# Moving the sum of two scaled token projections from VectorE to GpSimd in a fused decoder kernel

## The reference

```python
A = minimum(-softplus(dd_A), -A_FLOOR);  dt = softplus(dd_dt + dt_bias);  tr = sigmoid(trap)
theta = cumsum(tanh(angles) * dt * pi)            # one angle per head and rotated feature
def step(carry, (dt, A, tr, th, b, c, x)):        # over the 128 tokens
    alpha = exp(A * dt);  beta = (1 - tr) * dt * alpha;  gamma = tr * dt
    base = b * (px * beta + x * gamma)            # px is x of the token before
    sr = sr * alpha + [base[:R] * cos(th), base[R:]];   si = si * alpha + base[:R] * sin(th)
    y = sum((sr[:R] * cos(th) + si * sin(th)) * c[:R]) + sum(sr[R:] * c[R:])
out = (y + D * x) * silu(z) @ w_out.T
x1 = layernorm(u + out)
```

## Time and profile before

| | before |
|---|---|
| time, median of 3 runs | 638.13 us (637.15 to 638.27) |
| span of the profiled execution | 639.7 us |
| the seven groups that start at 46.4 us and end at 206.6 us | 160.2 us |
| mixer's last group, from 206.6 us to the end of its block | 19 us |
| attention and experts | from 226 us to 639.7 us |
| busy over the whole span: PE, DVE, ACT, POOL | 90%, 75%, 44%, 32% |

### The profile page before, as it was taken

One profiled execution on the slowest core, in us unless ns is written; L12 is line 12 of the kernel. 1 busy time (PEld: TensorE's weight loads), 2 busy tenths in 40 slices (PEclk: granted clock), 3 DMA queues, 4 the chain that ended last, 5 costly groups with the idle time before them and its releaser, 6 DMA issues. The chain is left out here.

```text
span 639.7 us, 17897 instructions
## 1 busy us (share of the span) xinstructions
PE 578.3 (90%) x6280; PEld 482.1 (75%) x6280; DVE 480.6 (75%) x1174; ACT 279.9 (44%) x548; POOL 205.7 (32%) x256
## 2 busy tenths in 40 slices
PE   5769998999999856998999999788999999999994
PEld 5647876777787645787788877576888888888884
DVE  2858878977988758686787788675887887887863
ACT  2356645645755423564575564353233233233220
POOL 4233214314412574324445547732021021020122
PEclk9969999999999976998999999899999999999998
DMA  7123122112111363445445645000010000110000
GB/s 223 61 68 86 40 66 66 36 63 66 53 55 40 106 190 105 132 138 148 140 131 149 166 117 168 13 5 34 1 34 2 33 33 0 33 33 0 18 18 16
DMA packets 43086, 46.13 MB, mean 72 GB/s; under 512 B 5056, under 2 KB 31328, under 8 KB 43024
## 3 DMA queue, kind: packets, MB, share of 16 engines
q1 hardware_dynamic: 41104, 42.57, 22.8%
q0 software_dynamic: 704, 1.92, 1.0%
q10 hardware_dynamic: 1216, 0.79, 0.5%
HBM read 32.48 MB, written 10.94 MB: 68 GB/s over the span
## 5 line engine op out<-in xcount | busy, mean ns | idle before, releaser
L1957 PE MATMUL bank<-xT_hl_c,w_up 128*128 128x512 f32 x432 | 118.1, 409 | 2.4 <-ACTq L67 2.4
L141 POOL TENSOR_TENSOR rstd<-mv,norm_c 128x4 f32<-128x4 f32 x24 | 5.2, 216 | 292.4 <-DVE mv L135 189.1
L1282 DVE TENSOR_REDUCE nmax<-bank 128x4 f32<-128x512 f32 x112 | 72.0, 685 | 22.9 <-PE bank L1439 21.5
L1879 ACT ACTIVATE sg<-bank 128x512 f32<-128x512 f32 x72 | 43.0, 597 | 105.0 <-PE bank L1957 103.1
L1186 ACT ACTIVATE prob<-bank 128x512 f32<-128x512 f32 x128 | 69.4, 594 | 42.9 <-PE bank L1439 36.5
L1957 PEld LDWEIGHTS bank<-xT_hl_c,w_up 128*128 128x128 f32 x432 | 76.1, 189 | 15.8 <-ACTq L67 2.6
L1973 PEld LDWEIGHTS bank<-w_down,hid 128*128 128x128 f32 x576 | 74.4, 191 | 6.0 <-issue 0.5
L1973 PE MATMUL bank<-w_down,hid 128*128 128x128 f32 x576 | 75.6, 275 | 0.0
L1429 PE MATMUL bank<-neg_i,mask 64*128 64x256 bf16 x512 | 51.5, 280 | 9.6 <-issue 3.2
L1912 DVE TENSOR_TENSOR gu<-sg,bank 128x512 f32<-128x512 f32 x64 | 43.8, 685 | 21.4 <-PE bank L1957 11.4
L1916 DVE TENSOR_TENSOR hid<-gu,bank 128x512 f32<-128x512 f32 x64 | 44.0, 687 | 6.5
(11 more groups left out here) (220 smaller groups left out, 1192.3 us busy)
## 6 DMA issues: line engine op xcount, KB each, us to landing
rows<-sum_rows_scratch SPq DMA_DIRECT2D x32, 256.0 KB, 3.2
k_stack<-k_scratch SPq DMA_DIRECT2D x32, 128.0 KB, 2.8
q_stack<-q_scratch SPq DMA_DIRECT2D x32, 128.0 KB, 2.8
k_scratch<-k_part SPq DMA_DIRECT2D x16, 192.0 KB, 2.3
q_scratch<-q_part SPq DMA_DIRECT2D x16, 192.0 KB, 2.4
x<-xT_in SPq DMA_DIRECT2D x8, 256.0 KB, 8.2
mask<-mask_in SPq DMA_DIRECT2D x8, 256.0 KB, 3.0
xres<-x_in SPq DMA_DIRECT2D x8, 256.0 KB, 3.7
```

The source lines that it names most:

```text
L1282: dve.tensor_reduce(nmax[:, b, 4 * u:4 * u + 4], (SS0, SS1)[n % 2][:, :].rearrange("p (i k) -> p i k", i=4), AX_X, ALU.max, negate=True).t ...
L1879: act.activation(sg[:, k, :], GG[k][:, :], ACT.Silu).then_inc(a_s.sem, 1)
L1957: mm = pe.matmul(bank[:, :], w_up[:, which, a, c, :], xT_hl[par][:, v, :], start=(n == 0), stop=(n == 2))
```

## The change

The scaling of the two projections stays with DVE, but writes into one of two buffers (`xg` gets a second one); the sum of the halves, `w_tok`, is made by POOL, in a function `inputs_of` of its own. PE's `tokens` waits for the scaling, PE's `back` for POOL's sum. POOL's order becomes, in groups 0 to 6: `steps_of(g+2)` (groups 0 to 5), sum of block 2, masks of blocks 0 to 2 of group g+1, sum of block 3, mask of block 3, sums of blocks 0 and 1 of group g+1, then the norm of group g, and in group 6 the fill of the key stack. In group 7: sum of block 2, third part of the first keys, sum of block 3, the two other third parts. The rounded angles (`whole`) lose their buffer and lie in that of the sines (`trig`), with one more wait of DVE for its own `rotate` of the group before.

```diff
-        ang, whole, frac = sb("ang", [P, 2, GT]), sb("whole", [P, 2, GT]), sb("frac", [P, 2, GT])
+        ang, frac = sb("ang", [P, 2, GT]), sb("frac", [P, 2, GT])
         trig = sb("trig", [P, 2, GT])
+        whole = trig
...
-        s_w = sem("w_ready", 2 * GS)
+        s_xg, s_w = sem("xg_ready", GS), sem("w_ready", GS)
...
             dve.wait_ge(s_ang.sem, s_ang.at(g, 1))
+            dve.wait_ge(s_prod.sem, s_prod.at(g - 1, 3))
             dve.tensor_scalar(whole[:, :, :], ang[:, :, :], ROUND, -ROUND, ALU.add, ALU.add).then_inc(s_whole.sem, 2)
...
-        xg = sb("xg", [P, 2, D_INNER])
+        xg = sb("xg", [P, 2, 2, D_INNER])
...
+            def inputs_of(g, b):
+
+                pool.wait_ge(s_xg.sem, s_xg.at(g, b))
+                pool.wait_ge(s_y.sem, s_y.at(g, b - 2))
+                pool.tensor_tensor(w_tok[:, b % 2, :], xg[:, b % 2, 0, :], xg[:, b % 2, 1, :], ALU.add).then_inc(s_w.sem, 1)
+
             def group(g, par, left):
                 if left == 2:
                     steps_of(pool, g + 2)
-                if left:
-                    for b in range(GS):
+                inputs_of(g, 2)
+                if left:
+                    for b in range(GS - 1):
                         causal(pool, g + 1, b)
+                else:
+                    part_third(pool, a, 0, 1)
+                inputs_of(g, 3)
+                if left:
+                    causal(pool, g + 1, GS - 1)
+                    for b in range(2):
+                        inputs_of(g + 1, b)
                     if left == 2:
                         pool.wait_ge(s_frac.sem, s_frac.at(g + 2, 1))
                     normalise_pool(pool, g, s_res, s_x1, res, mv, rstd, norm_c, x1[:, bass.ds(g * GS, GS), :])
                 if not left:
-                    for group_, which in ((0, 1), (0, 0), (1, 1)):
+                    for group_, which in ((0, 0), (1, 1)):
                         part_third(pool, a, group_, which)
...
             for b in range(2, GS):
                 causal(pool, 0, b)
+            for b in range(2):
+                inputs_of(0, b)
             pairs(pool, group)
...
             def inputs_of(g, b):
 
                 dve.wait_ge(s_xx.sem, s_xx.at(g, b))
-                dve.wait_ge(s_w.sem, s_w.at(g, 2 * b - 1))
-                dve.tensor_tensor(xg[:, :, :].rearrange("p s (h e) -> p (s h) e", h=HEADS),
+                dve.wait_ge(s_w.sem, s_w.at(g, b - 2))
+                dve.tensor_tensor(xg[:, b % 2, :, :].rearrange("p s (h e) -> p (s h) e", h=HEADS),
...
-                                     [P, 2 * HEADS, HD]), ALU.mult).then_inc(s_w.sem, 1)
-                dve.wait_ge(s_w.sem, s_w.at(g, 2 * b))
-                dve.wait_ge(s_y.sem, s_y.at(g, b - 2))
-                dve.tensor_tensor(w_tok[:, b % 2, :], xg[:, 0, :], xg[:, 1, :], ALU.add).then_inc(s_w.sem, 1)
+                                     [P, 2 * HEADS, HD]), ALU.mult).then_inc(s_xg.sem, 1)
...
-                pe.wait_ge(s_w.sem, s_w.at(g, 2 * b - 4))
+                pe.wait_ge(s_xg.sem, s_xg.at(g, b - 2))
...
-                pe.wait_ge(s_w.sem, s_w.at(g, 2 * b + 1))
+                pe.wait_ge(s_w.sem, s_w.at(g, b))
```

More of the change, by code:

```diff
@@ L540, in _ @@
             def _(pool):
-                for s in (s_sel, s_turns):
+                for s in (s_sel, s_turns, s_w):
                     s.prime(pool)
@@ L618, in link @@
                     dve.wait_ge(s_dve, steps[0])
-                for s in (s_lo, s_prod, s_w, s_mix, s_yg, s_whole, s_frac):
+                for s in (s_lo, s_prod, s_xg, s_mix, s_yg, s_whole, s_frac):
                     s.prime(dve)
```

## The result

The changed kernel takes 646.08 us (median of 4 runs, 645.5 to 646.95) against 638.2 us (4 runs, 637.15 to 639.15) for the one before: a ratio of 1.0122 with an interval of 1.0106 to 1.0138, 7.9 us slower. The forecast was 636.6 us with a range of 634.2 to 640.0. The profiled execution took 646.06 us with a span of 644.3.

What follows compares the result with a forecast made beforehand. PE was taken as the bound in groups 0 to 6, held in two places by VectorE's queue. Gains of 5.0 us less 3.5 at the hand-over gave 638.2 of span, 636.6 us as median, range 634.2 to 640.0.

Steps and rivals of the forecast that it cites:

- Edits at nothing: Second `xg` buffer and shared `whole`/`trig` buffer: their added waits, on events most of a group back, were put at nothing.
- the sum behind it: Whole span: -5.0 us in the mixer's groups plus 3.5 at the hand-over, -1.5 us on 639.7.
- the two stops: PE's idle ahead of `features` and of `back(2)`: shorter by 0.25 and 0.54 us in each of groups 1 to 5.
- The wait for `c_rot`: PE's `features` after `rotate`: 0.3 us of idle expected to remain, where they stood 0.60.
- The price of the sum: One 256-column sum on GpSimd: 0.63 us from a line between two rows, bounds 0.32 and 1.05.
- The slack of 0.07 us: At `back(2)`: GpSimd's sum seen at 7.27 us, PE arriving at 7.34, so the sum is hidden.
- 0.85 us a sum: Rival 1, GpSimd bounding `back(2)`: about this price turns gain to loss; 640.7 us at 1.05 a sum; chance 0.15.
- Group 7, 3.5 us: Hand-over to attention: norm and fill behind the sums delay the second keys' store by 3.5 us, bounds 2.8 and 4.3.
- Rival 2: Hand-over: the second keys' store does not hold the block or attention has slack; only gain remains, 633.1 us; chance 0.12.
- rival 3: PE's stops move instead of going, residual no earlier, `features` wait as before: 3.5 us against 3.5, 638.1 us; chance 0.23.
- The distance of 1.6 us between span and median: Runs' median 638.13 lay 1.6 us below the profiled span of 639.7; kept to turn 638.2 into 636.6.
- 0.7 us for when the clock returns: TensorE's clock around the hand-over, where PE's stop gets longer: an allowance of 0.7 us either way.

Runs made afterwards that it cites:

- the better order: GpSimd's fill moved ahead of group 7's first sums, group 6's norm behind block 3's sum, against the changed kernel with 37 memsets: 633.01 us.
- the twin with the other order on GpSimd: Kernel before, sums left on VectorE, with only GpSimd's norm and fill moved in the last two groups: 638.82 us, ratio 1.0011.
- 37 memsets: Changed kernel plus 37 one-column memsets in VectorE's early idle stretch, putting its later code back at its old places: 638.06 us, ratio 1.0006.
- slot 0: VectorE's experts' loop jumped to the start of a 256-instruction block: 639.36 us on the changed kernel, 635.61 with GpSimd's new order and no memsets.
- slot 239: Kernel before, with VectorE's experts' loop moved by a jump to this place in a block of 256 instructions: 644.23 us, ratio 1.0091.
- slot 111: Changed kernel, with VectorE's experts' loop moved by a jump to this place in a block of 256 instructions: 644.78 us, ratio 1.0105.
- slot 106: Changed kernel with GpSimd's new order, no memsets, VectorE's experts' loop moved by a jump to this place in a block of 256: 642.66 us.
- the eight memsets: Changed kernel with GpSimd's new order and 8 memsets in place of 37, no jump: 634.36 us, ratio 0.9927.
- slots 100 and 106: Changed kernel with GpSimd's new order, no memsets, VectorE's experts' loop jumped to either place in a block of 256: 636.59 and 642.66 us.

## Why the prediction was wrong, step by step

- **"Edits at nothing", and the sum behind it.** This is the step that failed. That paragraph puts two added waits at nothing and names no other edit; the sum then has terms for the mixer and the hand-over only, as the text ahead of it says that "the change lies in the mixer alone". It has no term for what 37 instructions fewer do to the code behind them. The runs showed two stops of VectorE at the returns of the experts' loop, 5.44 and 5.14 us, and 9.9 us more in that stage. Most of the miss is there: in the profile 646.1 less 9.9 is 636.2, and with the code back in its place the median is 638.06, 8.0 us less. Between that and the forecast of 636.6 stay 1.5 us, for which see the last point. No rival named the place of the code, so the range did not hold the time either.
- **Groups 0 to 6, 4.8 us by the two stops, and 0.2 more at the start of group 7:** 4.55 measured, in part by luck. Groups 1 to 5 became shorter by 0.67 to 0.74 us each (0.79 forecast), group 0 by 0.54 (0.8), and group 6, which counted as 0, by 0.46. Both stops were where the rows showed them. The waits for `mix` are gone, and in group 0 `back` now waits 0.46 us for GpSimd's sum. The wait for `c_rot` (0.3 us expected) is gone in group 0, is 0.37 to 0.40 us in three groups, and stays at 0.72 and 0.74 in two, where it was 0.58 to 0.66 before. As forecast, `frac` no longer runs beside the steps: its longest went from 1786 to 1226 ns. The lower bound of the 5.0 us was added up wrong: 5 x 0.42 + 0.8 + 0.2 is 3.1, not 3.3.
- **The price of the sum, 0.63 us:** 0.73 measured. The line was drawn between two rows of different kinds. The 64-column row adds two full operands; the one at 512 columns reads its second as one number for each 128 columns. Rows of the same kind are now there: 0.32 for 64, 0.46 for 128, 0.73 for 256 columns, about 2.1 ns a column, by which 512 would be 1.3 us (an estimate), not 1.05. The Trainium skill (page GPSIMD Engine Reference, section "Engine selection") says about twice VectorE's time for two inputs: here it is 0.73 to 0.42, 1.7 times.
- **The slack of 0.07 us, and 0.85 us a sum as the point where gain turns to loss:** too strict. At 0.87 us the seven groups keep 4.4 us of the gain (160.23 less 155.79), which is more than the 3 us that the hand-over took; at 1.16 they keep 1.6 (160.23 less 158.64), which would be less. Both were measured with the better order, so the net times of these prices in the changed kernel's order are argued.
- **Group 7, 3.5 us:** 2.98 measured, and the chain is the one named: norm, fill, sum, third part, store, landing. Rival 2 (covered) and rival 3 (the stops move) did not come true.
- **The distance of 1.6 us between span and median:** misread. In every run here the time is the span and 1.7 to 1.8 us (644.3 and 646.06, 637.3 and 639.07, 631.3 and 633.01). The profiled execution of before thus took about 641.4 us (an estimate), 3 above the median; its attention took 211.35 us where the twin with the other order on GpSimd took 208.62. Taking differences saved the sum, but levels read in that profile were 3 us high.
- **The worth of the change without its place, -1.5 us:** the stages show it (155.71 + 24.36 against 160.23 + 21.31 us is -1.47), the times do not: 638.06 us, with an interval from 1.3 us below to 2.0 above the kernel before. One thing speaks for a loss behind the mixer: in both profiles TensorE's clock fell at the hand-over, where PE had been busy 1.1 and 1.7 of the 5 us from 222 to 227; with 37 memsets it was still at its lower level (1.2 GHz) between 232 and 237 us, where the kernel before had the full one again (2.4 GHz):

```profile
232.00:237.00 5.00, 3.49 (x61) 2.96 (x56) 4.57 (x8) 1.86 (x4) 5.00 (x4) 1.00 0.56 158
```

```profile
232.00:237.00 5.00, 4.32 (x42) 3.34 (x39) 4.93 (x10) 0.83 (x2) 4.85 (x5) 0.50 0.45 139
```

(Window, length, busy us of PE, PEld, DVE, ACT and POOL with counts, granted clock, DMA share, GB/s; first before, then with 37 memsets.) I had allowed 0.7 us for when the clock returns. But the same two profiles do not show the loss in the attention's row (209.92 us with 37 memsets, 211.35 before, 208.62 in the twin). The runs point the same way as the clock: its mean is 0.965 over the 10 runs with 37 memsets, 0.967 over the 10 of the changed kernel at slot 0, 0.971 over the 53 of the kernel before that ran beside the experiments, and 0.970 over the 5 with 37 memsets and the better order. What the clock costs in the mean of runs stays open.

## What to carry to other kernels

An edit that changes the number of an engine's instructions moves all its later code. Where a later loop's body is longer than two pieces of 128 instructions, as these 281 are, look at the rows at the loop's return ("issue" ahead of the first instruction of a turn, more packets on the instruction queue) before judging the edit, and give the loop's head a place of its own. Take an unexpected difference to the table of stages first: a stage whose code did not change and whose time did is where to look. And work moved to a side engine is hidden only as long as what is queued behind it there is not on a chain to the end.

## What was not expected of the hardware

- A return of a loop on VectorE whose body of 281 instructions reaches into a fourth piece of 128 costs 3.0 to 5.4 us of standing still (5.44 and 5.14 in the changed kernel, 3.02 and 3.18 at slot 239, 3.01 twice at slot 111, 4.01 and 3.74 at slot 106), with some 10 packets of 8 KB more over two returns. That the changed kernel's own body reaches into a fourth piece is inferred from the eight memsets; its slot was not read. The edge is bracketed by slots 100 and 106 only, and why the stop differs from place to place was not tried.
- Where the body ends in the third piece, the return costs 0.46 to 0.55 us, and the whole stage has 4 to 7 packets.
- A jump to slot 0 or 100, taken once, goes with 1.5 to 2.2 us more in the stage (201.9 to 202.6 against 200.4); a kernel without a jump had 1.3 more (201.7), so the price is not exact.
